# Work around the first expert tiles moved between ScalarE, VectorE, GpSimd and TensorE in an adaLN attention and mixture-of-experts kernel

## The reference

```python
mod = (silu(c) @ wmod).reshape(8, 6, 1, 128)      # sa, ca, ga, sb, cb, gb
h = layernorm(x) * (1 + ca) + sa
x = x + ga * attention(h)                         # 16 heads of 8, causal, inner layernorm, Wo
h = layernorm(x) * (1 + cb) + sb
x = x + gb * ffn(h)
# ffn, for every token:
bids = sigmoid(h @ conf_w.T + conf_b) * wealth    # 8 experts
best two bids -> routing weights softmax(bid1, bid2)
out = sum over the two experts of weight * ((silu(h @ gate_w.T) * (h @ up_w.T)) @ down_w.T)
```

## Time and profile before

| | before |
|---|---|
| median of 3 executions | 612.96 us (611.4 to 614.01) |
| profiled execution, its own time | 611.13 us |
| span of its profile | 609.4 us |
| TensorE matmul busy | 552.1 us, 91% |
| VectorE busy | 470.1 us, 77% |
| ScalarE busy | 404.2 us, 66% |
| GpSimd busy | 244.4 us, 40% |
| mean granted clock of TensorE | 0.966 |

### The profile page before, as it was taken

One profiled execution on the slowest core, in us unless ns is written; L12 is line 12 of the kernel. 1 busy time (PEld: TensorE's weight loads), 2 busy tenths in 40 slices (PEclk: granted clock), 3 DMA queues, 4 the chain that ended last, 5 costly groups with the idle time before them and its releaser, 6 DMA issues.

```text
span 609.4 us, 16545 instructions
## 1 busy us (share of the span) xinstructions
PE 552.1 (91%) x5257; PEld 416.9 (68%) x5258; DVE 470.1 (77%) x1593; ACT 404.2 (66%) x715; POOL 244.4 (40%) x328
## 2 busy tenths in 40 slices
PE   5787999999999999999999989999889999999920
PEld 2464555666566566575666549998779999999920
DVE  5899778889899899898998757875846666667635
ACT  4424788888878888788778876765445656565511
POOL 5401301041453643535535345666553333333326
PEclk9597999999999999999999999999999999999975
DMA  4441576732242332333331011122422211111147
GB/s 124 133 139 53 152 209 178 206 98 81 72 123 83 89 105 81 114 88 94 109 98 55 16 42 42 41 58 65 109 67 54 54 44 51 46 46 51 36 176 250
DMA packets 61511, 56.82 MB, mean 93 GB/s; under 512 B 11156, under 2 KB 55572, under 8 KB 61444
## 3 DMA queue, kind: packets, MB, share of 16 engines
q1 hardware_dynamic: 56548, 44.88, 26.6%
q0 software_dynamic: 4320, 8.99, 4.7%
q10 hardware_dynamic: 576, 2.10, 0.9%
HBM read 36.92 MB, written 18.45 MB: 91 GB/s over the span
## 4 chain that ended last, share of the span: by engine, by line
PE 75%; DVE 7%; issue 5%; DMA 4%; ACT 3%; POOL 2%; SPq 1%; another core or an unknown queue 1%; POOLq 0%; ACTq 0%; DVEq 0%
PE psN L970 16%; PE psO L570 13%; PE psO L981 8%; PE psT L551 8%; PE psN L536 7%; PE psT L553 5%; PE psN L538 5%; PE psM L578 2%; DMA probs<-expert_out 2%; DVE negm L1415 1%; PE psM L596 1%; PE psM L601 1%; PE psM L644 1%; PE psM L606 1%; PE psT L957 1%
## 5 line engine op out<-in xcount | busy, mean ns | idle before, releaser
L1415 DVE TENSOR_REDUCE negm<-psN 128x1 f32<-128x512 f32 (+3 forms) x352 | 210.9, 636 | 31.5 <-PE psN L538 27.2
L1098 ACT ACTIVATE probs<-psT 128x512 f32<-128x512 f32 x320 | 180.4, 595 | 40.4 <-PE psT L553 32.1
L970 PE MATMUL psN<-probs 128*128 128x128 f32 x1136 | 139.5, 275 | 0.7 <-issue 0.4
L970 PEld LDWEIGHTS psN<-probs 128*128 128x128 f32 x1136 | 132.6, 192 | 1.6 <-issue 1.5
L2177 POOL DMA_INDIRECT expert_out<-kst_all,dest x71 | 69.1, 973 | 108.2 <-DVE kst_all L1932 98.5
L536 PE MATMUL psN<-kst_all,qst_all 74*128 74x256 bf16 (+2 forms) x384 | 101.2, 281 | 6.2 <-DVE negm L1415 4.1
L551 PE MATMUL psT<-qst_all,kst_all 74*128 74x256 bf16 (+2 forms) x384 | 99.7, 277 | 1.6 <-DMA qst_all<-mrow 0.6
L570 PE MATMUL psO<-probs,vaug 128*32 128x512 f32 (+3 forms) x1024 | 93.7, 444 | 0.1
L538 PE MATMUL psN<-kst_all,qst_all 117*128 117x128 bf16 x512 | 91.7, 222 | 0.0
L1292 ACT ACTIVATE probs<-gu_w 128x1024 f32 x70 | 74.0, 1057 | 24.8 <-PE psN L970 20.0
L1908 DVE TENSOR_TENSOR probs<-probs,psN 128x512 f32<-128x512 f32 x71 | 48.7, 686 | 53.4 <-PE psN L970 22.7
(11 more groups left out here) (242 smaller groups left out, 739.5 us busy)
## 6 DMA issues: line engine op xcount, KB each, us to landing
qst_all<-q_parts_dram SPq DMA_DIRECT2D x96, 96.0 KB
kst_all<-k_parts_dram SPq DMA_DIRECT2D x96, 96.0 KB
kst_all<-dispatched SPq DMA_DIRECT2D x71, 66.0 KB
q_parts_dram<-qparts SPq DMA_DIRECT2D x24, 128.0 KB
k_parts_dram<-kparts SPq DMA_DIRECT2D x24, 128.0 KB
xall<-in_x SPq DMA_DIRECT2D x8, 256.0 KB, 3.4
gu_w<-in_gateT SPq DMA_DIRECT2D x4, 512.0 KB, 5.1
gu_w<-in_upT SPq DMA_DIRECT2D x4, 512.0 KB, 4.9
```

The costliest lines, as they stand in the source:

```text
L970: mm = pe.matmul(bank[par][:, c * P:(c + 1) * P], ew[par][:, half, c * P:(c + 1) * P], xgT[par], start=True, stop=True)
L1098: nc.scalar.activation(probs[:, g % 2, 512 * u:512 * (u + 1)], psT[:, u % TBANKS, :], ACT.Exp, scale=SOFTMAX_SCALE).then_inc(exp_done, 1)
L1415: nc.vector.tensor_reduce(dst, src, axis=AX.X, op=ALU.max, negate=True).then_inc(nat_done, 1)
```

## The change

Nothing of the computation changes but one function: the exp of batch 7's bid difference becomes the power e^d. The parts:

1. **ScalarE's start.** The norm of batch 6 (`h_norm(L - 1)`, four instructions), of which two stood in the last step and two behind it, goes behind `silu` of tile 0. The Silu table is loaded right behind the last exps, and `keep_values(7, 3)` follows.
2. **TensorE's start.** The last part of the values (`values(7, 3, 3)`) goes behind the transpose of tile 0.
3. **VectorE's start.** `keep_tile(0, 0)` goes ahead of `normalise(7, 2)` and waits for all values (`pv_done`). The pads' four instructions leave VectorE.
4. **Pads by GpSimd**, behind its last step, ahead of `h_scale` of batch 6. `h_shift` of batch 6 goes ahead of `o_inv` of batch 7. SyncE waits for `pads_set`.
5. **keep_z.** That of batch 6 goes ahead of `silu` of tile 6 (it stood behind it); that of batch 7 goes from behind `silu` of tile 10 to ahead of that of tile 11, behind a copy of weights.
6. **Batch 7 scaled by VectorE.** Its `h_scale` and `h_shift` go from GpSimd (at tile 6) to VectorE (at tile 9, ahead of links 10 to 15 of batch 6).
7. **The last router power by GpSimd.** `exp_bids(7)` leaves ScalarE (it stood behind `silu` of tile 14) and becomes `exp_of_bids`, a power with the constant e, on GpSimd at tile 15; a memset of `euler` at the program's start makes the constant.

The diff's core:

```diff
 sync, pads_out_of:
-                    sp.wait_ge(dispatch_ready, 1)
+                    sp.wait_ge(pads_set, 4)
...
 tensor:
-            for c in range(1, TB):
+            for c in range(1, TB - 1):
                 values(L, 3, c)
...
             turn_in(0, 0)
+            values(L, 3, TB - 1)
...
 scalar:
-                    if has_batch(b - 1):
+                    if has_batch(b - 1) and b < B - 1:
                         h_norm(b - 1, (0,))
                         h_norm(b - 1, (1,))
...
             all_steps(step)
-            h_norm(B - 2, (2, 3))
             nc.scalar.preload_act_table(ACT.Silu)
             keep_values(B - 1, 3)
...
+                if j == 0:
+                    h_norm(L - 1)
...
-                if j == 6:
-                    keep_z(L - 1)
...
                     exp_bids(L - 1)
-                    keep_z(L)
-                if j == 14:
-                    exp_bids(L)
...
                 keep_weights(*divmod(j + 1, U))
+                if j == 6:
+                    keep_z(L - 1)
+                if j == 11:
+                    keep_z(L)
                 silu(*divmod(j, U))
...
 vector:
-                    if b == B - 1:
-                        dve.wait_ge(t_full, UNITS * (STEPS - 1))
-                        link(V.memset(padrows[:, :, 0:C_E0], 0.0))
-                        link(V.memset(padrows[:, :, C_E0], -1.0))
-                        link(V.memset(padrows[:, :, C_W0:], 0.0))
-                        V.tensor_copy(padrows[:, :, C_TOK], padtok[:]).then_inc(dispatch_ready, 1)
...
-            normalise(L, 2)
...
                 if j == 9:
+                    dve.wait_ge(xr_ready, L + 1)
+                    V.tensor_tensor(xn2[:], xn2[:], modbc[:, L, 2:3, :].broadcast_to([P, TB, E]), ALU.mult
+                                    ).then_inc(h2_chain, 1)
+                    dve.wait_ge(h2_chain, L + 1)
+                    V.tensor_tensor(rows_of(L)[:, :, 0:E], xn2[:], modbc[:, L, 1:2, :].broadcast_to([P, TB, E]), ALU.add
+                                    ).then_inc(h2_ready, 1)
                     for i in range(10, 16):
                         route(L - 1, i)
...
+            dve.wait_ge(pv_done, TB * STEPS)
             keep_tile(0, 0)
+            normalise(L, 2)
...
 gpsimd:
+            gp.memset(euler[:], math.e).then_inc(f_zero, 1)
...
+            gp.memset(padrows[:, :, 0:C_TOK], 0.0).then_inc(pads_set, 1)
+            gp.memset(padrows[:, :, C_E0], -1.0).then_inc(pads_set, 1)
+            gp.memset(padrows[:, :, C_W0:], 0.0).then_inc(pads_set, 1)
+            gp.tensor_copy(padrows[:, :, C_TOK], padtok[:]).then_inc(pads_set, 1)
             h_scale(L - 1)
+            h_shift(L - 1)
             o_inv(L)
-            h_shift(L - 1)
+            def exp_of_bids(b):
+                pool.wait_ge(r_chain, LINKS * b + 16)
+                gp.tensor_tensor(edbid[:], euler[:], dbid[:], ALU.pow).then_inc(ed_ready, 1)
...
-                if j == 6:
-                    h_scale(L)
-                    h_shift(L)
+                if j == 15:
+                    exp_of_bids(L)
```

More of the change, by code:

```diff
@@ L1 @@
+import math
 from contextlib import ExitStack
@@ L149, in adaln_attention_moe @@
         neghalf = sb("neghalf", [P, B, TB])
+        euler = sb("euler", [P, TB])
         identf = sb("identf", [P, P])
@@ L227, in adaln_attention_moe @@
             sem("r_chain"), sem("ed_ready"), sem("slot_full"), sem("count_full"))
-        head_counted, ew_first = sem("head_counted"), sem("ew_first")
+        head_counted, ew_first, pads_set = sem("head_counted"), sem("ew_first"), sem("pads_set")
         dispatch_ready, tiles_ready, pads_out = sem("dispatch_ready"), sem("tiles_ready"), sem("pads_out")
@@ L485, in pads_out_of @@
                 if e == 0:
-                    sp.wait_ge(dispatch_ready, 1)
+                    sp.wait_ge(pads_set, 4)
                     sp.dma_start(xd[NX * REGION:XROWS, :].rearrange("(n p) c -> p n c", p=P), padrows[:, NX:, :]
                                  ).then_inc(pads_out, 16)
-                    sp.wait_ge(dispatch_ready, 2)
+                    sp.wait_ge(dispatch_ready, 1)
                 row = sp.value_load(padslots[0:1, e:e + 1], min_val=0, max_val=XROWS - P)
@@ L2127, in _ @@
             gp.memset(onesrow[:], 1.0).then_inc(f_const, 1)
+            gp.memset(euler[:], math.e).then_inc(f_zero, 1)
             gp.memset(ones[:], 1.0).then_inc(f_zero, 1)
-            pool.wait_ge(f_zero, 1)
+            pool.wait_ge(f_zero, 2)
             gp.affine_select(out=before_t[:], in_=ones[:], compare_op=ALU.is_ge, fill=0.0, base=-1,
```

## The result

The changed kernel takes 613.97 us (median of 22), the kernel before 612.05 beside it (median of 22): ratio 1.0027, interval 1.0016 to 1.0038. That is slower by 1.7 us, inside the 0.5% called no change, where 2.3 us of gain were forecast, and above the range. The profiled execution took 614.47.

A forecast was written before the change was run, and what follows sets the result against it. TensorE was taken as the limit in settled tiles, at 2.79 us a tile, with time lost around the seam. Gains of 1.5 + 0.9 - 0.1 = 2.3 us took the median from 612.96 to 610.6 us; range 607.6 to 613.4.

The forecast's parts named there:

- The seam: Between attention and tiles: multiply(0) 3.0 us earlier, shrinking to 1.5 us won at the copy of tile 2.
- the block: At weights(0), VectorE stands until GpSimd's shift of batch 6 ends, costing 1.5 us of the 3.0 gained.
- tiles 8 to 10: TensorE stands 0.8 us before batch 7's transpose, saves as much at tile 8's down; 0.9 us gained in all.
- the wait for the counts: TensorE's wait of 0.61 us ahead of the rank matmul goes away, part of the 0.9 us gained.
- The last power: Around tiles 15 to 16: 1.3 us from saved table loads given back as VectorE waits for GpSimd's power; 0.1 lost.
- Rival (b): Between tiles 14 and 28, late TensorE results with unnamed reasons swallow the gain; 612.6 us, chance 0.15.

The follow-up runs named there:

- shift_behind: Changed kernel with GpSimd's shift of batch 6 moved back behind o_inv of batch 7; 612.79 us, ratio 1.0024 to the kernel before.
- 611 sets: Sets of measurements in which the kernel before takes 611 to 612 us: the result and three sets of follow-up experiments.
- scatter_late: Changed kernel with one scatter of batch 5 moved on GpSimd from tile 7 to tile 8, behind the send of tile 7; 613.07 us, ratio 1.0025.
- scale_tile8: Changed kernel with scaling and shift of batch 7 on VectorE at tile 8, not tile 9; 609.11 us, ratio 0.9964; repeated 596.18 us, ratio 0.9927.
- 600 sets: Sets of measurements in which the same kernel before takes 600 to 601 us: two sets of follow-up experiments.
- set 1: First set of follow-up experiments, one of the 611 sets; the kernel before took 611.44 us (35 runs).
- seam_only: Kernel before with only the parts around tile 0 (parts 1 to 4 of the change); 612.43 us, ratio 1.001.
- power_scalar_2: Changed kernel with the last router power back on ScalarE; 613.17 us, ratio 1.0033; the same program in one of the 600 sets 597.57 us, ratio 0.995.
- set 3: Third set of follow-up experiments, one of the 600 sets, with unchanged kernels measured again; the kernel before took 600.75 us (23 runs).
- before_again: The kernel before, unchanged, measured again in set 3; 600.47 us, ratio 0.9998.
- scale_gpsimd: Changed kernel with scaling and shift of batch 7 back on GpSimd at tile 6; 611.04 us, ratio 0.9994.

## Why the prediction was wrong

**The seam: right in its mechanism, and in its sum by luck.** Forecast 3.0 less 1.5; measured 1.46 at tile 2, because two errors of 0.6 cancel. The gain ahead of the block was 2.4 (363.17 for 365.54), since the values came at 360.48 and not at 359.93, and the block cost 0.9 (shift_behind), not 1.5.

**The failed step is that on tiles 8 to 10**, in the prediction's words: "the shift is done at 394.9, while TensorE's transpose of batch 7 stood at 394.13", so that TensorE "stands 0.8 us there, and saves as much" and 0.9 us are gained. With the seam's 1.46 taken off, the shift should have ended at 393.4; it ended at 395.95. VectorE began on time (389.20, forecast 390.7 less 1.46) and was through its five links at 390.31, but where the step lets `multiply(8)` follow at once it stood 2.52 us for TensorE's results. That wait the step put at nothing, because it did not ask what GpSimd does with the 2.5 us that the change frees. GpSimd filled them with issues: scatter, send, send, scatter, 1.3 us apart. In the 611 sets TensorE's results are not seen until up to 2.2 us after the start of the last of such a row (1.85 for up of tile 8). At tile 11 this step was 4.4 us off, 2.08 lost for 2.36 gained: 2.7 of it are the late shift, 1.4 the lower clock that follows TensorE's 3.62 us of idleness, 0.3 an issue gap. scatter_late moves the first of these by 0.93, and scale_tile8 wins 4.3 of the 4.4 back (399.85 for 404.15 at tile 11). In the 600 sets the term was smaller than forecast as well: TensorE stood 1.01 and 0.41 there, not 0.8, while the wait for the counts did go.

**The clock.** The prediction has no such term; the trace of before held none between 55 and 587 us. The changed kernel's has two stretches, 1.4 us each. More of it shows in the runs: mean clock 0.958 in the median over 22 runs, 0.964 in the kernel before (35 runs of set 1), where the 7 runs at 0.967 or more have a median of 609.9 us and the 4 at 0.961 or less 614.5. But among the changed kernel's own 22 runs the clock does not order the times: the 6 at 0.962 or more have a median of 614.3, the 12 at 0.957 or 0.958 one of 614.2. So its price rests on the rows of the profiled runs. In seam_only one stretch took more than the seam's gain of 1.5.

**The last power: right in size, for a reason not given.** Forecast 0.1 lost; power_scalar_2 and the changed kernel differ by less than can be measured in a 611 set; by the rows at tile 16 TensorE's late result covers VectorE's wait. In the 600 sets, where nothing covers it, the power on GpSimd costs 0.8 by the traces; the intervals of the two ratios, 0.995 and 0.9963, overlap.

**The sum.** Seam 1.5 won; then, instead of 0.9 won, 3.5 lost; and 1.2 more behind tile 11, where the stretch at 434 costs 1.4: 3.3 us slower in the profiled runs (614.47 for 611.13), 1.7 by the interval's ratio. Rival (b) named the right place, results that come late for reasons unknown, but as something that swallows a gain, not as something that a freed GpSimd makes worse. In the 600 sets the ratio is 0.9963; the forecast was 610.6 / 612.96 = 0.9962. That is partly luck: the seam's 1.5 is there, but in the two traces of set 3, about 1.1 us of the 1.5 won between tiles 8 and 11, and 0.5 in tile 11, come from a stretch at the lower clock in before_again (399.58), and tiles 11 to 29 gave back 0.3 all the same.

**Open.** What makes a set a 611 or a 600 set: the results name the same chip for set 1 as for set 2, the programs are the same, and up to tile 0 the traces of either kind differ by some 1 us. One more difference stands in the traces: those of the 611 sets hold 10,471 to 11,069 records of semaphore updates, those of the 600 sets 12,395 to 12,621 (the changed kernel's 10,965 and 12,421), most of the missing ones of DMAs that land. Whether the recording has a part in the holds no run tests, nor whether the matmul or only its signal is late. Why the clock falls at 399 in seam_only, after idle times of 0.81 and 0.86, and not in the kernel before after 0.82 and 0.61, is open too: in before_again the same program idles 0.83 and 0.62 there, and the clock falls.

## What to carry to other kernels

When work leaves an engine that also issues indirect DMAs, ask what its queue does with the room: here, in the 611 sets, four issues closed up, and ScalarE, VectorE and in the end TensorE itself waited for TensorE's results. A wait that a change puts in an engine's order belongs where that engine stands idle already (VectorE at tile 8), not one tile later. And compare kernels in sets of both kinds before a 0.3% verdict is believed: the same change was 1.0027 and 0.9963.

## What the runs showed that was not expected

- **Rows of indirect DMAs hold TensorE's results.** In the 12 traces of 611 sets, 5 to 15 `silu` a trace (tiles 3 to 70) start over 1 us behind gate's record with ScalarE idle, up to 4.2 behind. Of the 101, 88 start while the last issue is the third or a later one of a row (each under 1.5 us behind the one before; a row that grows during the wait counts). In the 8 traces of 600 sets there is none. After a hold, results of two tiles arrive within 0.3 us. Between the two traces of the kernel before, 611.13 and 601.61 us, 8 of the 9.5 us lie where the holds are: from tile 9 to 29 it takes 72.1 us in its first trace and 64.2 in before_again's. The Trainium skill (Perfetto Trace Analysis, Summary: the profiler window per engine type) says that a matmul's recorded end is an estimate and that the semaphore's way is not in the record; the trace agrees, and here the hidden part is 0.04 us as a rule and up to 4.2 in a hold.
- **The clock falls after short waits too.** 3.62 us of idleness came before one fall, but 0.38 and 0.42 before another (scale_gpsimd). The Trainium skill (TensorE: Matmul & The Clock Gate, HAM oscillation) names waits between bursts of matmuls as the cause; the first fall agrees, the second that section does not explain.
- **A blocked VectorE instruction, undone.** The add with two SBUF inputs took 1.05 us under GpSimd's shift and 0.16 with the shift elsewhere, and 1.26 where the shift went.
